# Gate/up and down as seven block products for eight, in groups of 1024 tokens with act kept in HBM

## Chip, cores and metric
One Trainium2 chip, one core. The metric is the device time of one execution, in microseconds; the kernel before has a median of 2003.85 us over three runs (2000.64 to 2003.87).

## What is computed
x has 2048 tokens of 1024 elements, in 8 sequences of 256. Each sequence has its own low-rank adapter (rank 16 of 16 sets). All is f32. The result is x + ffn(cond(x)):
```
gate = x @ Wg.T + 0.5 * (x @ Ag.T) @ Bg.T        # Wg: 2752 x 1024, per sequence Ag, Bg
up   = x @ Wu.T + 0.5 * (x @ Au.T) @ Bu.T
act  = silu(gate) * up                           # 2048 x 2752
y    = act @ Wd.T + 0.5 * (act @ Ad.T) @ Bd.T    # 2048 x 1024
top  = top_k(y @ W_gate + b_gate, 2)             # of 8 experts
out  = x + mean over the two of relu(y @ W_e[e] + b_e[e])
```

## The kernel before
The precision of f32 comes from splitting each operand into a high part (rounded to TensorE's fast f32 form, on ScalarE) and a low part (operand less high part, on VectorE): every block product is three matrix products, high x high, high x low and low x high (`first`, lines 1001 to 1003, and `mm3`, lines 953 to 955). A "product" below is one such TensorE instruction of 128 rows and 512 columns.

Four groups of 512 tokens (`NG`) follow one another. In gate/up, 22 chunks of 128 rows of Wg and Wu (`first`) are multiplied with x of the group, 8 blocks of 128 along the depth, 24 products to a chunk; the last chunk of each, 64 rows, shares one. x, split, stays in SBUF (`x_t`), and so does act of the group (`act_t`). ScalarE takes silu (L549), VectorE multiplies (L562), ScalarE and VectorE split act (L573, L582). Adapter products have 256 columns: `lora_in` (L962, 32 per group), `lora_out` (L974, 88), `lora_down_in` (L1022, 86). In down (`down`), two halves of 512 output columns each go over 11 weight pieces for four blocks of 128 tokens. y goes to HBM by `store_y`.

Weights come in pieces of 128 x 1024 (512 KB): SP's queue loads them into three raw buffers (`load`, L232), ScalarE writes the high part into a ring of three (`split_hi`, L456), VectorE the low part (`split_lo`, L475). The ring is free again when TensorE has done with the piece (`s_pe`).

Logits of y: VectorE multiplies y by broadcast rows of the gate matrix and accumulates (`l_step`, L640), 64 steps of 512 columns per group, the last group 32; for the rest TensorE transposes four tiles (L1085) and multiplies them with the matrix (L1095). VectorE then picks the two experts, ranks of the first 12 token blocks are made early (`early_hots`), and the expert stage runs over blocks of 128 rows sorted by expert (`one`): 48 products and 8 transposes (L1143) a block, GpSimd gathers y (L380), takes the low part of the transposed block (L390), adds the bias (L400) and scatters (L408). Expert weights are split by VectorE into one of two sides of R (L944, L945); those of expert 0 and three pieces of expert 1 are split in the last group (`EARLY`).

The order on ScalarE, VectorE and GpSimd is made by `Jobs`: each job has a key, the number of the weight piece at which it is due, and the engine runs them in order of key. An engine that waits in one job holds all that follow.
```
    def run(self, eng):
        for _, _, fn, args in sorted(self.jobs, key=lambda j: j[:2]):
            fn(eng, *args)
```


## Time and profile before

| | us |
|---|---|
| median of three runs | 2003.85 |
| span of the profiled execution, first to last instruction | 1998.1 |
| profiled execution's own time | not given apart; one of 2000.64, 2003.85 and 2003.87 |
| TensorE busy | 1971.3 (99%) |
| VectorE, ScalarE, GpSimd busy | 889.5, 629.5, 498.1 |
| HBM read and written, MB | 248.75, 36.70 |

The page comes from one execution. A busy share is a mean over stages; a TensorE duration is that of one instruction from its start to its modelled end, and overlaps with the next. The distance between starts is what an instruction costs. The granted clock of 1.0 is 2.4 GHz.

### The profile page before, as it was taken

The page shows a single profiled execution, that of the slowest core. Times are in us where ns is not written, and L with a number is a line of the kernel's source. Part 1 is how long each engine was busy: PE and PEld are TensorE (multiplying, and loading weights), DVE is VectorE, ACT ScalarE, POOL GpSimd, SP SyncE. Part 2 cuts the span into 40 slices and gives each one's busy share as a digit, 9 for nine tenths or more (in the row PEclk, how much of TensorE's full clock was granted, in tenths as well). Part 3 has the DMA queues.
Part 4 walks back from the last instruction along what each step waited for, and adds up shares of the span by engine and source line. Part 5 has one row for each costly group of instructions (what it writes and reads, how often), then busy time and mean ns, then how long its engine had stood idle before and what let it go on. Part 6 is the DMA issues. An engine that isn't in the chain of part 4 may idle for free.

```text
span 1998.1 us, 24457 instructions
## 1 busy us (share of the span) xinstructions
PE 1971.3 (99%) x9247; PEld 1644.4 (82%) x9247; DVE 889.5 (45%) x1293; ACT 629.5 (32%) x775; POOL 498.1 (25%) x373
## 2 busy tenths in 40 slices
PE   8999999999999999999999999999999999999997
PEld 6888888888888888888888888888888788888886
DVE  4333343255555423555553255555656443444310
ACT  4332332233233322323333232232332233333332
POOL 3111100011111001111110021111001666666664
PEclk9999999999999999999999999999999999999999
DMA  6433335344333442444344345433454566766543
GB/s 194 140 122 106 112 129 165 99 138 161 122 121 124 140 143 90 156 159 128 119 138 146 116 136 160 128 119 114 161 186 148 131 185 179 188 182 176 154 98 59
DMA packets 82802, 278.19 MB, mean 139 GB/s; under 512 B 11760, under 2 KB 12144, under 8 KB 82544
## 3 DMA queue, kind: packets, MB, share of 16 engines
q1 hardware_dynamic: 59472, 197.53, 30.2%
q0 software_dynamic: 23216, 79.05, 15.1%
q8 instruction: 82, 1.34, 0.3%
q14 instruction: 32, 0.26, 0.0%
HBM read 248.75 MB, written 36.70 MB: 143 GB/s over the span
## 4 chain that ended last, share of the span: by engine, by line
PE 98%; DVE 1%; issue 0%; DMA 0%; POOL 0%; SPq 0%; ACT 0%; POOLq 0%
PE PS L1002 16%; PE PS L1001 16%; PE PS L1003 16%; PE PS L953 14%; PE PS L955 14%; PE PS L954 14%; PE PS L974 2%; PE PS L1022 2%; PE PS L1143 2%; PE PS L962 1%; PE PS L1072 0%; PE PS L1050 0%; PE PS L1051 0%; DMA raw<-in_xp 0%; PE PS L1095 0%
## 5 line engine op out<-in xcount | busy, mean ns | idle before, releaser
L475 DVE TENSOR_TENSOR ring<-raw,ring 128x1024 fp32r<-128x1024 f32 x259 | 317.5, 1226 | 544.0 <-ACT ring L456 543.9
L1001 PE MATMUL PS<-R,ring 128*128 128x512 f32 x1376 | 538.3, 391 | 9.1 <-DVE R L468 6.4
L1002 PE MATMUL PS<-R,ring 128*128 128x512 f32 x1376 | 538.8, 392 | 0.0
L1003 PE MATMUL PS<-R,ring 128*128 128x512 f32 x1376 | 538.0, 391 | 0.0
L308 POOL DMA_INDIRECT AB<-in_bgu,idx_b x176 | 165.9, 943 | 898.7 <-DVE R L517 869.2
L456 ACT ACTIVATE ring<-raw 128x1024 fp32r<-128x1024 f32 x259 | 272.8, 1053 | 300.8 <-PE PS L955 292.0
L1001 PEld LDWEIGHTS PS<-R,ring 128*128 128x128 f32 x1376 | 259.4, 189 | 59.5 <-DVE R L468 6.4
L1003 PEld LDWEIGHTS PS<-R,ring 128*128 128x128 f32 x1376 | 259.0, 188 | 55.4
L1002 PEld LDWEIGHTS PS<-R,ring 128*128 128x128 f32 x1376 | 259.4, 188 | 49.1
L953 PE MATMUL PS<-ring,R 128*128 128x512 f32 x672 | 262.1, 390 | 0.0
L954 PE MATMUL PS<-ring,R 128*128 128x512 f32 x672 | 261.7, 389 | 0.0
L955 PE MATMUL PS<-ring,R 128*128 128x512 f32 x672 | 261.6, 389 | 0.0
L953 PE MATMUL PS<-R,ring 128*128 (+1 forms) x592 | 235.4, 398 | 2.5 <-issue 2.5
L955 PE MATMUL PS<-R,ring 128*128 (+1 forms) x592 | 231.9, 392 | 0.0
L954 PE MATMUL PS<-R,ring 128*128 (+1 forms) x592 | 231.4, 391 | 0.0
L573 ACT ACTIVATE R<-sbuf 128x512 fp32r<-128x512 f32 x88 | 55.6, 632 | 412.1 <-DVE sbuf L562 408.7
L944 DVE CAST R<-raw 128x1024 fp32r<-128x1024 f32 x53 | 66.1, 1246 | 200.0 <-PE PS L955 182.3
L640 DVE CUSTOM_DVE_ANT_0 PS<-ybuf,ytp 128x512 f32<-128x512 f32 x224 | 148.6, 719 | 0.0
L955 PEld LDWEIGHTS PS<-ring,R 128*128 128x128 f32 x672 | 126.1, 188 | 26.3
L954 PEld LDWEIGHTS PS<-ring,R 128*128 128x128 f32 x672 | 126.3, 188 | 26.0
L953 PEld LDWEIGHTS PS<-ring,R 128*128 128x128 f32 x672 | 126.2, 188 | 25.9
L953 PEld LDWEIGHTS PS<-R,ring 128*128 128x128 f32 x592 | 111.9, 189 | 25.6 <-issue 3.7
(152 smaller groups left out, 1704.5 us busy)
## 6 DMA issues: line engine op xcount, KB each, us to landing
raw<-in_wp SPq DMA_DIRECT2D x259, 512.0 KB, 3.5
raw<-in_we SPq DMA_DIRECT2D x64, 512.0 KB, 5.5
ytp<-in_wgb SPq DMA_DIRECT2D x56, 256.0 KB, 3.7
y_scratch<-ybuf POOLq DMA_DIRECT2D x7, 1024.0 KB, 6.7
raw<-in_xp SPq DMA_DIRECT2D x13, 512.0 KB, 3.6
AB<-in_be SPq DMA_DIRECT2D x8, 512.0 KB, 4.1
AB<-in_bgu,idx_b POOLq DMA_INDIRECT x176, 3.1
ybuf<-in_xp SPq DMA_DIRECT2D x2, 512.0 KB, 7.3
```

Source lines behind the costliest of these rows:

```text
L308: e.indirect_dma_start(out=braw[:, n % 2, b * 256:(b + 1) * 256], out_offset=None, in_=bgu, in_offset=ioa(idx_b[0:96, 2 * g + b, i:i + 1]) ...
L456: e.activation(piece_dst(i, 0), raw_t(i), ACT.Copy).then_inc(s_hi, 1)
L475: e.tensor_tensor(piece_dst(i, 1), raw_t(i), piece_dst(i, 0), ALU.subtract).then_inc(s_lo, 1)
L573: e.activation(act_t(c, 0)[0:p, :], sbuf2[0:p, 2 + c % 2, :], ACT.Copy).then_inc(s_ah, 1)
L640: e.tensor_tensor_reduce(out=PS[:, (5 if g < NG - 1 else 1) + n % 3, :], in0=ybuf[:, tt, h * 512:(h + 1) * 512], in1=ytp[:, (s % 2) * 512: ...
L944: link(e.tensor_copy(s_w_t(ex, k, 0), raw[:, i % RW, :]))
L953: e.matmul(out_, hi, whi, start=start, stop=False)
L954: e.matmul(out_, hi, wlo, start=False, stop=False)
L955: return e.matmul(out_, lo, whi, start=False, stop=stop)
L1001: e.matmul(PS[:, bank, :], w[0][:, sl], x_t(0, k), start=(k == 0), stop=False)
L1002: e.matmul(PS[:, bank, :], w[0][:, sl], x_t(1, k), start=False, stop=False)
L1003: e.matmul(PS[:, bank, :], w[1][:, sl], x_t(0, k), start=False, stop=False)
```

## The change
Two groups of 1024 tokens. Each is cut in two halves of 512 tokens, the depth of 1024 in two halves of 512, and the weight rows in pairs of chunks of 128. A pair of chunks with both token halves is a 2 x 2 by 2 x 2 block product, made with seven block products and sums of blocks (Winograd's form): `unit`. Even units are gate, odd ones up; unit 20 has gate and up of chunk 20. The 64 remaining rows go in plain products (`half_unit`).

A unit's made weight blocks S1 to S4 come from four GpSimd steps (`mix_w`); the made x blocks T1 to T4 of group 0 from VectorE and GpSimd at the start, those of group 1 through HBM (`mix`, four GpSimd steps in each of 14 rounds in units 3 to 16 of group 0, which also make four blocks of the down weights). Of the seven products each is accumulated into one of four PSUM banks; ScalarE copies a bank out (`e_copy`), TensorE goes on in it, VectorE adds (`c_add`).

act of a group has the same form in down: GpSimd makes four act blocks per pair of units (`mix_act`), seven are stored to HBM (`act_store`, on SP's queue) and come back as 35 pieces per group (`load_a`), split anew by ScalarE and VectorE (`a_hi`, `a_lo`). Down has seven stages (`STAGES`) of five pieces, 24 products each, and remainders of depth 192 in plain products (`rem`) in four of them. The down weights' low parts move from VectorE to GpSimd (`d_lo`).

The logits of the second 512 tokens of each group are made by TensorE with transposes and sums (`turn2`, `sum2`), 8 tiles of each; the first 512 stay on VectorE, 64 steps, in stages 2 to 5 (`l_key`). Stores of y, copies of x, and all other plain transfers are issued from SP's queue, which has an order by keys too. The keys now count block products: 228 to a group (`op`), gate/up at 0 to 149, down from 150 on, two to a piece. The weight ring has six slots of 512 columns. Of the expert weights only expert 0 is split early. In the diff, `st`, `tile`, `slot` and the like are buffers; `s_...` are semaphores.
```diff
-NG = 4
+NG = 2
 NC = 22
-NU = 65
-S2 = 43
+NP = 21
...
+OPS = 228
...
+D0 = 150
+NM = 39
+STAGES = 7
+FIRST_M = [0, 5, 11, 16, 21, 27, 33]
...
+        def load_a(e, j):
...
+            e.dma_start(raw_a(j), act_d[g, s, a].rearrange("p a n -> p (a n)")).then_inc(s_ra[jj % 3], 16)
...
+        def act_store(e, g, p):
...
+            for s, t, what, v in ((0, AT_T, s_mu, g * 44 + 4 * p + 1), (1, AT_T + 2, s_mu, g * 44 + 4 * p + 3),
+                                  (5, AT_T + 3, s_mu, g * 44 + 4 * p + 4), (3, SP_T, s_Sa, 4 * n + 1),
+                                  (6, AT_T + 1, s_Sa, 4 * n + 2), (2, SP_T + 1, s_Sa, 4 * n + 3),
+                                  (4, SP_T + 2, s_Sa, 4 * n + 4)):
+                e.wait_ge(what, v)
+                e.dma_start(act_d[g, s, p // 2, :, p % 2, :], tile(t)).then_inc(s_st, 16)
...
+        for j, (o, h) in enumerate([(0, 0), (0, 1), (2, 0), (2, 1), (1, 0), (1, 1), (3, 0), (3, 1)]):
+            sp.add(-29 + j, load_x0, o, h)
+        sp.add(-28.5, constants, False)
+        sp.add(-26.5, load, 1)
...
+            sp.add(7.0 * (r + 3) + 0.3, mix_load, r)
+            sp.add(7.0 * (r + 3) + 5.3, mix_store, r)
...
+                sp.add(op(g, 7 * (2 * p + 1)) + 11.3, act_store, g, p)
...
+        def l_key(g, o):
+            if o < 32:
+                return stage_end(g, 1) + 0.6 + 0.55 * o
+            return stage_end(g, 4) + 0.6 + 0.3 * (o - 32)
...
+        def mix_w(e, g, q):
...
+            if q:
+                e.wait_ge(s_lo, lo_of(g, 7 * (q - 1) + 5))
...
+            e.tensor_tensor(tile(S_T), a[1][0], a[1][1], ALU.add).then_inc(s_S, 1)
+            e.wait_ge(s_S, n + 1)
+            e.tensor_tensor(tile(S_T + 1), tile(S_T), a[0][0], ALU.subtract).then_inc(s_S, 1)
+            e.wait_ge(s_S, n + 2)
+            e.tensor_tensor(tile(S_T + 2), a[0][1], tile(S_T + 1), ALU.subtract).then_inc(s_S, 1)
+            e.tensor_tensor(tile(S_T + 3), a[1][0], a[0][0], ALU.subtract).then_inc(s_S, 1)
...
+        def mix_act(e, g, p):
...
+            e.wait_ge(s_mu, g * 44 + 4 * p + 4)
...
+            e.tensor_tensor(tile(SP_T), tile(AT_T + 1), tile(AT_T + 3), ALU.add).then_inc(s_Sa, 1)
+            e.wait_ge(s_Sa, n + 1)
+            e.tensor_tensor(tile(AT_T + 1), tile(AT_T + 1), tile(AT_T), ALU.subtract).then_inc(s_Sa, 1)
+            e.tensor_tensor(tile(SP_T + 1), tile(SP_T), tile(AT_T), ALU.subtract).then_inc(s_Sa, 1)
+            e.wait_ge(s_Sa, n + 3)
+            e.tensor_tensor(tile(SP_T + 2), tile(AT_T + 2), tile(SP_T + 1), ALU.subtract).then_inc(s_Sa, 1)
...
+        def mix(e, r):
+            e.wait_ge(s_cl, 64 * (r + 1))
+            e.tensor_tensor(st[0], st[1], st[0], ALU.subtract).then_inc(s_cp, 1)
...
+            e.tensor_tensor(st[1], st[1], st[3], ALU.subtract).then_inc(s_cp, 1)
...
+            e.tensor_tensor(st[3], st[3], st[0], ALU.subtract).then_inc(s_cp, 1)
...
+            e.tensor_tensor(st[2], st[2], st[3], ALU.subtract).then_inc(s_cp, 1)
...
+        def x0_t3(e, h):
...
+            e.wait_ge(s_xt, h + 1)
+            e.wait_ge(s_q[6 + h], 16)
+            e.tensor_tensor(X0[1][:, hs], X0[1][:, hs], X0[3][:, hs], ALU.subtract).then_inc(s_xp, 1)
...
+        def d_lo(e, g, m):
...
+            e.tensor_tensor(slot2(n, 1), pair(raw_t(i)), slot2(n, 0), ALU.subtract).then_inc(s_lp, 1)
...
+                pool.add(op(g, 7 * q) - 5.4, mix_w, g, q)
...
+                pool.add(op(g, 7 * (2 * p + 1)) + 8.4, mix_act, g, p)
...
+                pool.add(op_m(g, m) - 6 + 0.55, d_lo, g, m)
...
+            pool.add(7.0 * (r + 3) + 3.0, mix, r)
...
+            pool.add(-6 + 0.1 * h, x0_t3, h)
+            pool.add(-5.6 + 0.1 * h, x0_t4, h)
...
+        def w_hi(e, g, n):
...
+                e.wait_ge(s_S, (g * NP + q) * 4 + j - 1)
+            hi_free(e, op(g, n))
+            e.activation(slot(op(g, n), 0), w_src(g, n), ACT.Copy).then_inc(s_hi, 1)
+        def w_lo(e, g, n):
+            e.wait_ge(s_hi, g * (LO1 + 2 * NM) + n + 1)
+            e.tensor_tensor(slot(op(g, n), 1), w_src(g, n), slot(op(g, n), 0), ALU.subtract).then_inc(s_lo, 1)
...
+        def a_lo(e, j):
+            e.wait_ge(s_ah, j + 1)
+            e.tensor_tensor(a_ring(j, 1), raw_a(j), a_ring(j, 0), ALU.subtract).then_inc(s_al, 1)
...
+        def e_copy(e, g, q, k):
...
+            e.wait_ge(s_pe, pe_op(g, 7 * q + [0, 2, 3, 5][k]))
...
+            e.activation(tile(E_T + [0, 1, 2, 0][k]), PS[:, bk + [0, 2, 0, 0][k], :], ACT.Copy).then_inc(s_ec, 1)
...
+        def c_add(e, g, q, k):
...
+            e.tensor_tensor(c_tile(q, k), tile(E_T + [0, 2, 0, 1][k]), PS[:, bk + [1, 2, 3, 0][k], :],
+                            ALU.add).then_inc(s_c, 1)
...
+            e.tensor_tensor_reduce(out=JK[n % 2], in0=tile(SET_C + tt),
...
+                key = op(g, n) - 5.6
+                act.add(key, w_hi, g, n)
+                dve.add(key + 0.15, w_lo, g, n)
...
+                    act.add(n0 + [1.05, 3.05, 4.05, 6.05][k], e_copy, g, q, k)
...
+                    dve.add(due, c_add, g, q, k)
...
+            def lora1_in(g):
...
+                for w in range(2):
...
+                    src = ([("B11", 0), ("B21", 4)], [("T1", 0), ("B11", 0), ("B22", 4)])[w]
+                    for i in range(2):
...
+                        todo = [(o, k0, k, part) for o, k0 in src for k in range(4) for part in range(2)]
...
+            def unit(g, q):
...
+                main1(g, n0, "B11", bk, True, True).then_inc(s_pe, 1)
...
+                m = main1(g, n0 + 1, "B21", bk + 1, True)
...
+                main1(g, n0 + 2, "T1", bk + 2, True, True).then_inc(s_pe, 1)
...
+                if q == 0:
+                    lora1_in(g)
...
+                e.wait_ge(s_ec, ec + 1)
+                main1(g, n0 + 3, "T2", bk, False, True).then_inc(s_pe, 1)
...
+                e.wait_ge(s_ec, ec + 2)
+                main1(g, n0 + 4, "B22", bk + 2, False)
+                m = lora1_out(g, q, 0, 1, bk + 2)
...
+                e.wait_ge(s_ec, ec + 3)
+                main1(g, n0 + 5, "T3", bk, False, True).then_inc(s_pe, 1)
...
+                main1(g, n0 + 6, "T4", bk + 3, True)
+                e.wait_ge(s_ec, ec + 4)
+                lora1_out(g, q, 1, 1, bk)
+                lora1_out(g, q, 1, 0, bk + 3).then_inc(s_pe, 1)
...
+            def half_unit(g):
...
+                main1(g, 147, "B11", 4, True, True).then_inc(s_u1, 1)
+                main1(g, 147, "T1", 5, True).then_inc(s_pe, 1)
...
+                main1(g, 148, "B22", 5, False)
...
+                main1(g, 148, "B21", 4, False)
...
+            def piece(g, s, kp):
...
+                e.wait_ge(s_al, j + 1)
...
+                e.wait_ge(s_lp, g * NM + m_ + 1)
...
+                        m = mm3(PS[:, bank(s, i), :], a_ring(j, 0)[:, o:o + 128], a_ring(j, 1)[:, o:o + 128],
+                                slot(G + a, 0), slot(G + a, 1), start=(kp == 0 and a == 0),
+                                stop=(kp == 4 and a == 1 and s not in (1, 4, 5)))
...
+            def rem(g, s, i):
...
+                mm3(o, act20(0, w)[:, ts], act20(1, w)[:, ts], slot(G, 0), slot(G, 1), start=False)
+                e.matmul(o, act21(w)[:, ts], slot(G + 1, 0), start=False, stop=False, skip_group_check=True)
+                return e.matmul(o, act21(w)[:, ts], slot(G + 1, 1), start=False, stop=False, skip_group_check=True)
...
+            def tail2(g, s):
...
+                        e.wait_ge(s_ev, ev_of(g, 6, i))
...
+            for m in range(8):
+                sum2(1, m)
+                if m < 6:
+                    turn2(1, m + 2)
```

## Rows read from the trace of the kernel before

**Rows 1.** The page: busy time by engine, and the granted clock in 40 slices
```profile
PE 1971.3 (99%) x9247; PEld 1644.4 (82%) x9247; DVE 889.5 (45%) x1293; ACT 629.5 (32%) x775; POOL 498.1 (25%) x373
...
PEclk9999999999999999999999999999999999999999
```

**Rows 2.** The chain in order of time (start us, us, what)
```profile
17.97 3.81 PE PS L962 x32
...
1157.66 3.82 PE PS L962 x32
...
1590.10 0.87 PE PS L1143 x8
1601.90 0.87 PE PS L1143 x8
```

**Rows 3.** Order of time, TensorE: transposes, a sum, the first expert transposes
```profile
1531.60 0.60 PE L1085 MATMUL PS<-ident,ybuf 128*128 128x128 f32 x4
...
1535.06 0.96 PE L1095 MATMUL PS<-wg_s,ytp 128*128 128x8 f32 x8
...
1538.11 1.07 PE L1143 MATMUL PS<-ident,sbuf 128*128 128x128 f32 x8
```

**Rows 4.** Two stretches: busy us of each engine, clock, DMA share, GB/s
```profile
0.00:18.00 18.00, 8.93 (x26) 6.67 (x27) 9.48 (x14) 9.35 (x11) 8.77 (x12) 0.91 0.85 280
760.00:1140.00 380.00, 380.00 (x1768) 317.50 (x1768) 181.98 (x292) 116.16 (x152) 50.16 (x53) 1.00 0.41 133
```

**Rows 5.** Groups by line and shape, TensorE: busy us, mean ns, idle before
```profile
L1001 PE MATMUL PS<-R,ring 128*128 128x512 f32 x1376 | 538.3, 391 | 9.1 <-DVE R L468 6.4 <-DVE R L475 2.7
L974 PE MATMUL PS<-TT,R 96*128 96x256 f32 x352 | 69.5, 283 | 0.0
```

**Rows 6.** Groups by line and shape, the other engines
```profile
L475 DVE TENSOR_TENSOR ring<-raw,ring 128x1024 fp32r<-128x1024 f32 x259 | 317.5, 1226 | 544.0 <-ACT ring L456 543.9
L456 ACT ACTIVATE ring<-raw 128x1024 fp32r<-128x1024 f32 x259 | 272.8, 1053 | 300.8 <-PE PS L955 292.0 <-DMA raw<-in_wp 5.4 <-PE PS L1072 3.4
L640 DVE CUSTOM_DVE_ANT_0 PS<-ybuf,ytp 128x512 f32<-128x512 f32 x224 | 148.6, 719 | 0.0
L390 POOL TENSOR_TENSOR ring<-ytp,ring 128x1024 fp32r<-128x1024 f32 x36 | 88.4, 2456 | 45.6 <-ACT ring L720 45.4
L517 DVE TENSOR_TENSOR R<-AB,R 32x512 fp32r<-32x512 f32 x104 | 70.3, 680 | 3.1
L582 DVE TENSOR_TENSOR R<-sbuf,R 128x512 fp32r<-128x512 f32 x84 | 58.2, 693 | 58.7 <-ACT R L573 58.7
L562 DVE TENSOR_TENSOR sbuf<-sbuf,PS 128x512 f32<-128x512 f32 x84 | 57.8, 688 | 119.0 <-PE PS L974 118.8
L549 ACT ACTIVATE sbuf<-PS 128x512 f32<-128x512 f32 x84 | 50.2, 597 | 259.7 <-PE PS L974 259.7
L640 DVE DVE_READ_ACCUMULATOR2_ANT Lp<- 128x1 f32 x224 | 31.7, 141 | 0.0
```

**Rows 7.** Order of time, TensorE, the start
```profile
8.23 0.63 PE L1002 MATMUL PS<-R,ring 128*128 128x512 f32 x1
8.65 0.63 PE L1003 MATMUL PS<-R,ring 128*128 128x512 f32 x1
```

**Rows 8.** The page, DMA issues: KB each, median us to landing
```profile
raw<-in_wp SPq DMA_DIRECT2D x259, 512.0 KB, 3.5
```

**Rows 9.** Order of time, GpSimd and VectorE, around 1550 and 1716 us
```profile
1550.23 2.20 POOL L362 TENSOR_TENSOR ybuf<-ybuf,cf 128x656 bf16<-128x656 bf16 x1 [0.78 <-DVE ybuf L912]
...
1716.11 2.39 POOL L400 TENSOR_TENSOR sbuf<-sbuf,AB 128x1024 f32<-128x1024 f32 x1 [0.87 <-ACT sbuf L728]
1716.28 3.31 DVE L945 TENSOR_TENSOR R<-raw,R 128x1024 fp32r<-128x1024 f32 x1
```

**Rows 10.** Order of time, VectorE between expert 1 and expert 2
```profile
1572.94 1.23 DVE L945 TENSOR_TENSOR R<-raw,R 128x1024 fp32r<-128x1024 f32 x1
1596.50 0.69 DVE L944 CAST R<-raw 128x1024 fp32r<-128x1024 f32 x1 [22.33 <-PE PS L955]
```

More of the change, by code:

```diff
@@ new lines, in build @@
+        for i in range(i, len(pieces)):
+            _, e, k = pieces[i]
+            if (e, k) in ((1, 0), (1, 2)):
+                sp.add(keys[i], load_bias, k // 2)
+            if e >= 2 and k == 3:
+                sp.add(keys[i], load_bias, e)
+            sp.add(keys[i], load, i)
+        for h in range(2):
+            sp.add(op_m(0, 33) + 0.1, load_x1, h)
+        for j in range(70):
+            g, jj = divmod(j, 35)
+            m = FIRST_M[jj // 5] + jj % 5
+            sp.add(max(op_m(g, m) - 6 - 5.3, op(g, 144.4 if jj < 2 else 147.3)), load_a, j)
@@ L707, in blk_hi @@
+        for h in range(2):
+            dve.add(-4.5 + 0.01 * h, x0_t1, h)
+            dve.add(-3.5 + 0.01 * h, x0_t2, h)
+        for k in range(8):
+            act.add(keys[at["e", 0, k]], e_hi, k)
+            dve.add(keys[at["e", 0, k]] + 0.1, e_lo, k)
         def blk_hi(e, b):
@@ new lines, in early_table @@
+            def early_table():
+                e.wait_ge(s_ee, 1)
+                for t in range(ET):
+                    m = e.matmul(EP[:, 32:36], e_or[:, t, :], e_ob[:, t].rearrange("p a b -> p (a b)"),
+                                 start=(t == 0), stop=(t == ET - 1))
+                m.then_inc(s_ep, 1)
+            for g in range(NG):
+                for q in range(NP):
+                    unit(g, q)
+                half_unit(g)
+                for s in range(STAGES):
+                    for kp in range(5):
+                        piece(g, s, kp)
+                        if g == NG - 1 and s == 6 and kp == 1:
+                            early_ranks()
+                        if g == NG - 1 and s == 6 and kp == 3:
+                            early_table()
+                    if s in REM_M:
+                        tail2(g, s)
```

1624 lines of the change are left out of this document (1036 added, 588 removed).

## The prediction, made before the changed kernel was run
> **What bounds the kernel now.** I read the page first: the busy shares, the slices, then the chain that ended last. TensorE is busy for 99% of the span, its share is at 9 in all slices but the first and the last, and the granted clock stands at 1.0, the 2.4 GHz level, from end to end [rows 1]. The chain in order of time shows the period: the adapter product of a token group starts at 17.97 and, three groups on, at 1157.66, so a group takes 379.9 us, and the expert stage's first transposes start at 1538.1 [rows 3]. The table by stretches says that nothing but TensorE is near a limit: in a whole group it is busy for 380.0 of 380.0 us, VectorE for 182, ScalarE for 116, GpSimd for 50 [rows 4]. So time comes off only if TensorE gets less to do, and the question is whether the others can then still feed it.
>
> **TensorE's work.** A group of 512 tokens has 43 x 24 products of 512 columns in gate/up and 2 x (21 x 4 x 3 + 4 x 2 + 4) in down, 1560 in all, and 32 + 88 + 86 = 206 adapter products of 256 columns. 32 of the latter take 3.82 us, 0.119 each [rows 2]; (379.9 - 24.5) / 1560 = 0.2278 us per product of 512 columns. (The mean duration of 391 ns [rows 5] overlaps with the next one and is no price.)
> After, a group of 1024 tokens has 21 units of 7 x 12 products, 48 in the half unit, 7 x 5 x 24 in down, 4 x 4 x 5 for the remainders and 16 adapter outputs: 2748. Two groups have 5496 against 4 x 1560 = 6240: 744 fewer x 0.2278 = **-169.5 us**. Adapter products of 256 columns: 80 + 176 + 172 = 428 per group, 856 against 824, **+3.8**. Half of the logits leave VectorE's accumulating multiply for TensorE: 16 transposed tiles and sums against 4. One tile costs 0.60 for its transposes and 0.96 for its sum [rows 3]: 12 x 1.56 = **+18.7**.
>
> **The start.** Before, the adapter input begins at 17.97 behind 24 products (5.5 us), so the pace counts from 12.5. After, it stands behind three products, and the third (T1 times a made weight block) has a long way: GpSimd's queue holds both halves of T3 and T4 ahead of the first weight mix. Ten transfers of 512 KB come first; at the 280 GB/s of the first 18 us [rows 4] each takes 1.9, so x block 12 is whole at about 17 and block 22 at about 21. VectorE makes T1 (1.23 a half), GpSimd T3 (2 x 2.46), VectorE the low parts of T1 and B22 and then T2, GpSimd T4 (2 x 2.46) and then S1 [rows 6]; with VectorE and GpSimd excluding each other (below) I get 36 for S1, 38 for the third product, a pace that counts from 38 - 5.5 = 32.5, 20 us later than before. While TensorE had gaps before, the rows show products 0.43 apart instead of 0.23 (half clock, 1.2 GHz) [rows 7]; +2. **+22**. Bounds: 10 if nothing excludes anything and the transfers go faster; 35 with each half mix at the upper price below and a cold clock throughout.
>
> **Boundaries.** Group 1 starts only when all four sums of the last stage are out of PSUM: 4 x 0.69 behind the last product, where before the waits are in my 0.2278; the same at the end of group 1; with the first act blocks coming back from HBM (store, load of 3.5 us [rows 8], split of 1.05 and 1.23, all inside the 11.4 us of the half unit) I take **+5** (2 to 12). The first adapter outputs wait for four ScalarE copies of about 1 us and a VectorE step, with two products (5.4 us) as cover: **+2** for two groups. The end of group 1 has eight transposes and sums in a chain with ScalarE copies of 0.6: **+3** (1 to 8).
>
> **The lock between VectorE and GpSimd.** Here lies the risk. A VectorE subtraction of 1024 columns with both inputs in SBUF takes 1.23; the one that started 0.17 us behind a GpSimd one took 3.31: it stood until GpSimd's 2.39 were over [rows 9]. The Trainium skill (SBUF — State Buffer, "SBUF: two separate sides") calls this an exclusive lock on a shared port pair, held for the whole instruction, by GpSimd's operations and by VectorE's with two SBUF inputs. If it were no lock the next two paragraphs would cost nothing, and the sum would be 22 us lower; the row agrees with the lock. In the kernel before, GpSimd only gathers in this stage; after, it does the mixes of weights, of act and, in group 0, of the made operands, and half of the splits of down.
> Price of a 512-column step: VectorE 0.69 both ways, 0.68 for 32 partitions, ScalarE 0.60 [rows 6]. No row has GpSimd at 512 columns of f32. Below is half of 2.46, 1.2; above the 2.20 of 656 bf16 columns with a broadcast input [rows 9], 1.7 for 512. I take 1.31, half of 2.46 and the 0.08 that VectorE's half (0.69) has over half of its 1.23. The Trainium skill (GPSIMD Engine Reference, "Reconciling with measured numbers") gives 4.5 us at 2048 columns; with the row at 1024 that line would make it an estimated 1.33.
>
> **Gate/up units.** A unit lasts 84 x 0.2278 + 8 x 0.119 = 20.1 us. In it the lock is held by VectorE for 7 low parts, 2 gatings, 2 adapter rows (7.6) and by GpSimd for 4 weight mixes and 2 act mixes (7.9), in units 3 to 16 of group 0 for 4 more (13.1 in all, the sum 20.7). That is just over the unit. The order of the queues makes it sharper: ScalarE's split of the next unit's S1 is queued ahead of its copy of this unit's fourth product, and TensorE's sixth product waits for that copy. So S1 has to be there 12.9 us into the unit (5 products of 2.86, less 1.3 for split and copy). In even units GpSimd mixes act first: sums, adapter rows and gating end at 3.8, five GpSimd steps follow: 10.4 alone, 13.8 if each stands behind one VectorE step. I take half a microsecond for 20 even units and 2 more in the first group's busy ones, **+12** (0 to 121, below). Gathers are fewer (4 per pair of units for 2 per unit) and wider; GpSimd is busy with them for 50 of 380 us before [rows 4], and they fit.
>
> **Down.** A piece is 24 products, 5.5 us, 6.4 with adapter input; GpSimd's split takes 2.46, VectorE's 1.23, ScalarE's two 1.05 each: alone they fit. While logit steps run (0.72 under the lock and 0.14 [rows 6]; 32 are due in 52 us of stages 2 and 3, 32 in 32 us of stage 5) the lock is asked for 32 x 0.72 + 8.8 x 3.7 + 4.4 x 1.23 = 61 us of 52, and 23 + 5 x 3.7 = 41.5 of 32: some 9 us behind each time. Rings of three give a VectorE split 8.5 us of slack (two pieces less its own steps). So the stall is small: 2.5 in each of four windows, **+10** (0 to 50).
>
> **The expert stage** keeps its 11.8 us per block [rows 2]. It has three fewer pieces of expert 1 split beforehand, some 3 x 3 us on VectorE; it now ends them at 1574 and then idles 22.33 us until expert 0 is done [rows 10]. Covered, 0. The early ranks take VectorE 6 us inside two pieces (10.9): 0. Copying x is moved to SP's queue, ahead of loads with 9 us or more of slack: 0. HBM traffic: 86 MB of weights (164 pieces of 0.524) for 136 (260 pieces), and new are act out and in (73 MB) and the made operands (29 MB), 52 MB more over some 1440 us, 36 GB/s on top of 133 [rows 4], and about 225 in the busiest units against 280 shown: 0.
>
> **Sum**: -169.5 + 3.8 + 18.7 + 22 + 5 + 2 + 3 + 12 + 10 = -93 on a span of 1998.1. The profiled execution's own time isn't given apart; the median is 5.75 above the span, and I take that as what lies around it: 1905.1 + 5.75 = **1911 us**.
>
> **Rivals.** (a) The covers hold: no unit stalls, no window stalls, start +15: -122, **1882**. For it: all averages but one are below their limits. Against: the order in even units. (b) The forecast. (c) The lock costs more than my middle, the units 40 and the windows 30: -45, **1959**. (d) Slower: GpSimd's step is at its 1.7. Then S1 is ready at 3.8 + 5 x (1.7 + 0.69) = 15.8, 2.9 late in 20 even units, 58, and the busy units ask for 17 + 7.6 = 24.6 us of lock in 20.1, 4.5 x 14 = 63: 121 for the 12, so +16, **2020**. It decides from a step of about 1.65 us. Against it: a GpSimd step of 1024 f32 columns at 2.39, with nothing broadcast. That the seven products aren't a real saving is ruled out by the count. (e) No change needs 93 us of further stalls by chance.
> The chances: (a) 0.28, (b) 0.40, (c) 0.19, (d) 0.11, (e) 0.02. The range reaches from (a) with its best start, 1862, through (c) to 1970. About 0.2%, 4 us, is what a measurement of this kernel can tell from no change: faster 0.87, same 0.02, slower 0.11. The likeliest case alone: 1890 to 1935.
>
> **What would show it.** TensorE with 5496 products of 512 columns at 0.228 apart; the adapter input of group 0 starting at about 41; units of 20 to 21 us in group 1, up to 23 in the even units 4 to 16 of group 0; GpSimd's 512-column steps at 1.3; VectorE subtractions of 0.69 stretched to about 2 beside GpSimd; TensorE's waits put down to ScalarE's copies and low parts; the first expert transposes at about 1445. I am wrong if units are at 24, if TensorE's clock leaves 1.0 in gate/up, or if transfers are what ends its waits.

## The result and the profile after

The change makes the kernel slower: 2059.82 us (median of four runs, 2055.79 to 2063.94) against 2002.24 (2000.33 to 2003.87), ratio 1.0289, 95% interval 1.0270 to 1.0309. I had said 1911, 1862 to 1970. In the profiled executions the span goes from 1998.1 to 2060.6, up by 62.5 where my sum had it down by 93: the miss is 155 us. (By the medians it is 149: the profiled execution, 2062.44, is 1.8 above its span, where I had put 5.75.)

The page of the kernel after (busy time; clock in 40 slices; chain by engine and line):
```profile
PE 1882.0 (91%) x8679; PEld 1560.7 (76%) x8679; DVE 1141.9 (55%) x1355; ACT 744.0 (36%) x1054; POOL 1083.1 (53%) x659
...
PEclk8899999999899998899999999899998899999999
...
PE 66%; DVE 7%; issue 6%; DMA 6%; POOL 5%; ACT 3%; SPq 0%; ACTq 0%; DVEq 0%; POOLq 0%
```
TensorE has less to do, as forecast, but is busy for 91% instead of 99% [rows 1], its clock has dips, and the chain now leads through every engine and the DMA. Four stretches, with the columns of [rows 4]: the start, units 8 and 9 of group 0, and unit 18 of group 1:
```profile
0.00:18.00 18.00, 5.52 (x13) 3.91 (x13) 9.17 (x13) 6.44 (x7) 6.21 (x10) 1.00 0.82 319
...
242.40:268.80 26.40, 23.06 (x95) 18.67 (x94) 19.25 (x18) 9.27 (x16) 21.56 (x16) 0.87 0.83 301
268.80:288.90 20.10, 20.10 (x95) 16.76 (x94) 12.54 (x14) 7.92 (x14) 14.08 (x10) 1.00 0.50 171
...
1233.20:1253.80 20.60, 20.40 (x94) 16.70 (x93) 14.80 (x16) 8.97 (x16) 14.59 (x10) 1.00 0.48 160
```
Unit 9, at 268.8, takes 20.1 us, what I worked out for 84 products and 8 adapter products: the arithmetic saved is real. Unit 8, at 242.4, takes 26.4, TensorE idle for 3.3 of it and at a mean clock of 0.87. So I cut the trace at the first product of 512 columns of each unit and piece; such a table says where the time went:

| stretch, us | after | best of the runs below |
|---|---|---|
| group 0, unit 0 | 68.4 | 51.5 |
| group 0, units 1 to 20 | 458.4 | 402 |
| group 1, unit 0 | 60.8 | 51.5 |
| group 1, units 1 to 20 | 415.9 | 402 |
| two half units | 44.7 | 25.7 |
| stage 3's first piece and stage 5's remainder, both groups | 68.3 | 28.8 |
| the rest of down | 453.5 | 443 |

(The right-hand column isn't free of waits: the two units 0 would take 29.6 and 42.1 by the count of products alone, an estimate from 0.2278 and 0.119 us each and, in group 1, eight tiles of logits at 1.56.) Five kinds of wait make the difference. **Even units of group 0**; order of time on GpSimd, ScalarE, TensorE in unit 8:
```profile
242.83 1.62 POOL L653 TENSOR_TENSOR FT<-FT 128x512 f32<-128x512 f32 x1
247.19 0.90 POOL L691 DMA_INDIRECT brw<-in_bgu,idx_b  x1 [2.74 <-DVE R L975]
...
255.34 1.15 ACT L970 ACTIVATE R<-brw 96x512 fp32r<-96x512 f32 x2 [2.56 <-DMA brw<-in_bgu,idx_b]
256.39 0.57 ACT L1029 ACTIVATE FT<-PS 128x512 f32<-128x512 f32 x1
...
257.11 0.77 PE L1571 MATMUL PS<-R,ring 128*128 128x512 f32 x1 [3.34 <-ACT FT L1029]
257.67 0.63 PE L1572 MATMUL PS<-R,ring 128*128 128x512 f32 x1
258.10 0.63 PE L1573 MATMUL PS<-R,ring 128*128 128x512 f32 x1
```
ScalarE's copy of the third block product (L1029) has its input from about 251, but stands in the queue behind the adapter rows' splits (L970), which wait for gathers issued at 247.2 and 248.4, behind GpSimd's mixes and a wait for VectorE; the second landed 6.9 us later. TensorE needs those rows only at the end of the fifth block product, the copy at its start. And behind its wait its products stand 0.43 us apart (1.2 GHz) instead of 0.23.

**Unit 20 and the half unit** (ScalarE, then TensorE): the same with act's first piece, which comes back from HBM:
```profile
533.52 1.06 ACT L849 ACTIVATE R<-FT 128x1024 fp32r<-128x1024 f32 x1 [3.81 <-DMA FT<-act_scratch]
536.46 0.63 ACT L1062 ACTIVATE FT<-FT 128x512 f32<-128x512 f32 x1 [1.89 <-DVE FT L1057]
537.00 0.58 ACT L1029 ACTIVATE FT<-PS 128x512 f32<-128x512 f32 x1
...
537.63 1.23 PE L1616 MATMUL PS<-R 96*128 96x256 f32 x4 [6.38 <-ACT FT L1029]
```
**Group 1's unit 0** (ScalarE, TensorE): T4 back from HBM ahead of a logit copy (L1166):
```profile
843.45 2.00 ACT L880 ACTIVATE R<-raw 128x1024 fp32r<-128x1024 f32 x2 [10.28 <-DMA raw<-xt_scratch]
845.36 0.58 ACT L1166 ACTIVATE ytp<-PS 128x512 f32<-128x512 f32 x1
...
845.99 1.88 PE L1829 MATMUL PS<-wg_s,ytp 128*128 128x8 f32 x8 [9.23 <-ACT ytp L1166]
```
**The start** (TensorE, GpSimd). The third product starts at 38.83, where I had 38. But then there is a second wait, behind the second half of the adapter rows (ScalarE waits 10.3 us for their gather) and the copies queued after them, and later GpSimd stands still for 22.7 us behind the store of an adapter row that it gathers by way of HBM:
```profile
38.83 0.80 PE L1571 MATMUL PS<-R,ring 128*128 128x512 f32 x1 [17.92 <-DVE ring L834]
...
68.09 0.77 PE L1571 MATMUL PS<-R,ring 128*128 128x512 f32 x1 [11.39 <-issue]
...
89.58 0.94 POOL L680 DMA_INDIRECT ytp<-in_agu,idx_a  x1 [22.69 <-DMA ad_scratch<-ytp]
```
**The windows of the logit steps** (chain in order of time): two of the logit steps (L1205), 0.69 us each alone, take 2.8 and 3.1 beside GpSimd's splits, and the adapter's low part (L1011) is queued behind all of them:
```profile
769.67 2.83 DVE FT L1205
...
774.34 3.10 DVE FT L1205
...
784.92 0.69 DVE R L1011
785.61 0.04 issue
785.65 2.08 PE PS L1789 x4
```
The groups of the other engines show the lock [rows 6, 9] in its means: splits of act pieces take 2236 ns instead of 1226, of weight blocks 982 and 1065 instead of 693; GpSimd's four weight steps take 1.43 to 1.71:
```profile
L834 DVE TENSOR_TENSOR ring<-FT,ring 128x512 fp32r<-128x512 f32 x168 | 164.4, 982 | 180.3 <-ACT ring L830 177.7
L853 DVE TENSOR_TENSOR R<-FT,R 128x1024 fp32r<-128x1024 f32 x70 | 156.5, 2236 | 186.7 <-ACT R L849 186.5
L834 DVE TENSOR_TENSOR ring<-raw,ring 128x512 fp32r<-128x512 f32 x130 | 138.3, 1065 | 121.9 <-ACT ring L830 121.5
...
L626 POOL TENSOR_TENSOR FT<-raw 128x512 f32<-128x512 f32 x42 | 71.7, 1706 | 0.0
...
L621 POOL TENSOR_TENSOR FT<-raw 128x512 f32<-128x512 f32 x42 | 60.2, 1433 | 176.3 <-DMA raw<-in_wp 149.9 <-issue 20.6 <-DVE ring L834 5.7
```

### The profile page after: what moved, and what is told of

Read it like the earlier page. It is cut to its first block, busy times and chain, and to the rows that moved or that the text cites. A ratio compares the mean times of both kernels' runs of the same rounds, so it can differ in the third digit from the quotient of the medians.

```text
span 2060.6 us, 24701 instructions
## 1 busy us (share of the span) xinstructions
PE 1882.0 (91%) x8679; PEld 1560.7 (76%) x8679; DVE 1141.9 (55%) x1355; ACT 744.0 (36%) x1054; POOL 1083.1 (53%) x659
## 4 chain that ended last, share of the span: by engine, by line
PE 66%; DVE 7%; issue 6%; DMA 6%; POOL 5%; ACT 3%; SPq 0%; ACTq 0%; DVEq 0%; POOLq 0%
PE PS L1571 20%; PE PS L1572 19%; PE PS L1573 19%; DVE FT L1205 3%; DMA brw<-in_bgu,idx_b 3%; PE PS L1878 2%; PE PS L1616 2%; PE PS L1710 1%; DMA ytp<-in_wgb 1%; POOL brw L691 1%; DMA raw<-in_wp 1%; ACT R L970 1%; PE PS L1829 1%; ACT R L849 1%; DVE R L853 1%
## 5 line engine op out<-in xcount | busy, mean ns | idle before, releaser
L1571 PE MATMUL PS<-R,ring 128*128 128x512 f32 (+1 forms) x1800 | 724.9, 403 | 83.6 <-DVE ring L834 30.4
L1572 PE MATMUL PS<-R,ring 128*128 128x512 f32 (+1 forms) x1800 | 715.1, 397 | 0.0
L1573 PE MATMUL PS<-R,ring 128*128 128x512 f32 (+1 forms) x1800 | 714.1, 397 | 0.0
L1571 PEld LDWEIGHTS PS<-R,ring 128*128 128x128 f32 x1800 | 346.8, 193 | 161.4 <-issue 52.8
L1573 PEld LDWEIGHTS PS<-R,ring 128*128 128x128 f32 x1800 | 346.1, 192 | 75.6
L1572 PEld LDWEIGHTS PS<-R,ring 128*128 128x128 f32 x1800 | 347.6, 193 | 66.4
L712 POOL TENSOR_TENSOR ring<-raw,ring 128x1024 fp32r<-128x1024 f32 x78 | 192.5, 2467 | 360.6 <-ACT ring L840 357.5
L834 DVE TENSOR_TENSOR ring<-FT,ring 128x512 fp32r<-128x512 f32 x168 | 164.4, 982 | 180.3 <-ACT ring L830 177.7
L853 DVE TENSOR_TENSOR R<-FT,R 128x1024 fp32r<-128x1024 f32 x70 | 156.5, 2236 | 186.7 <-ACT R L849 186.5
L830 ACT ACTIVATE ring<-FT 128x512 fp32r<-128x512 f32 x168 | 105.9, 631 | 300.0 <-PE PS L1616 130.1
L834 DVE TENSOR_TENSOR ring<-raw,ring 128x512 fp32r<-128x512 f32 x130 | 138.3, 1065 | 121.9 <-ACT ring L830 121.5
L840 ACT ACTIVATE ring<-raw 128x1024 fp32r<-128x1024 f32 x78 | 82.7, 1061 | 334.2 <-PE PS L1573 309.7
L1571 PEld LDWEIGHTS PS<-ring,R 128*128 128x128 f32 x592 | 113.5, 192 | 44.2 <-DVE FT L1151 18.6
L975 DVE TENSOR_TENSOR R<-brw,R 32x512 fp32r<-32x512 f32 x88 | 99.3, 1148 | 69.2 <-ACT R L970 68.1
L1573 PEld LDWEIGHTS PS<-ring,R 128*128 128x128 f32 x592 | 113.1, 191 | 24.5
```

Of the source, the lines that this page charges most:

```text
L712: e.tensor_tensor(slot2(n, 1), pair(raw_t(i)), slot2(n, 0), ALU.subtract).then_inc(s_lp, 1)
L830: e.activation(slot(op(g, n), 0), w_src(g, n), ACT.Copy).then_inc(s_hi, 1)
L834: e.tensor_tensor(slot(op(g, n), 1), w_src(g, n), slot(op(g, n), 0), ALU.subtract).then_inc(s_lo, 1)
L840: e.activation(slot2(n, 0), pair(raw_t(i)), ACT.Copy).then_inc(s_hi, 2)
L853: e.tensor_tensor(a_ring(j, 1), raw_a(j), a_ring(j, 0), ALU.subtract).then_inc(s_al, 1)
L975: e.tensor_tensor(m, b_raw(p, t)[32:64], m, ALU.subtract).then_inc(s_bl, 1)
```

## Experiments

Three theories: A, the order of the queues; B, the lock and GpSimd's steps; C, transfers. "Dense" is the start of the last remainder of group 1, the last point before the expert stage: 1581.8 after the change. It matters because the runs on 16 columns leave out arithmetic, compute other logits and so have one or two expert blocks fewer (8623 and 8567 TensorE instructions for 8679, 56 to a block; the expert stage takes 446.4 and 436.7 us for 459.9). The time that a theory gave is set beside theirs with those 14 or 23 us added; for the rest only their dense part is compared.

### One thing at a time
**Adapter rows' splits later**
```diff
-  key = op(g, 14 * p) + [[-1.6, 2.6], [0.1, 2.6]][t][w]
+  key = op(g, 14 * p) + [[-1.6, 3.1], [0.1, 3.1]][t][w]
```


> One number: from the second pair of units on, the splits of the adapter rows of the T path (ScalarE and VectorE) are queued at 3.1 instead of 2.6 products into the even unit, so behind ScalarE's copy of the third product and no longer ahead of it. Nothing else moves. Theory A (order of the queues): in group 0 TensorE's wait in even units is that copy, held up behind a row gather that lands late; the fifth product needs the rows only at its end. Then the excess of units 1 to 20 of group 0 over 20.08 us falls from 57 us to about 30, and the time from 2060 to about 2025. Theory B (the lock between VectorE and GpSimd): what is late are the split weights themselves; the copy was only the first to show it. Then the units stay within 0.5 us of what they are and the time at 2055 to 2065. Theory C (transfers): the gathers land late because HBM and queues are full; the excess falls as in A, but landings stay at 7 to 8 us.

2051.58 us; dense 1571.8, 10 less. Units 1 to 20 of group 0 fall from 458.4 to 449.4. The copy is no longer late, and the low part of the rows (L975) takes its place, 0.9 to 1.3 us in most even units and 6.5 in unit 12: the gather itself is late. 9 us of the 27 that A promised in these units.

**GpSimd on 16 columns**
```diff
+  c = 16 if n else 512
...
-  e.tensor_tensor(tile(S_T), a[1][0], a[1][1], ALU.add).then_inc(s_S, 1)
+  e.tensor_tensor(tile(S_T)[:, 0:c], a[1][0][:, 0:c], a[1][1][:, 0:c], ALU.add).then_inc(s_S, 1)
...
```


> Leaves out most of the arithmetic: every two-input step of GpSimd before the expert stage (weight mixes, act mixes, made operands, low parts of the down weights) works on 16 columns of each 512 instead of all, but for the first unit's weight mix. Instructions, waits, transfers and queue orders are the same. It takes GpSimd's load and with it the lock away, and nothing else. Theory B (the lock is the cause of all): VectorE's steps are back at 0.69 and 1.23, units of both groups at 20.1, half units at 12, no window stalls; only the start and the act round trip stay: 1895 to 1910. Theory A (order of the queues is the cause, the lock its trigger): the even units of group 0 are at 20.1 to 20.6 too, since the gathers are then issued in time, but unit 20, the half unit and the stage with 32 logit steps in 27 us keep part of their waits, since there a load stands ahead in a queue: 1920 to 1950. Theory C (transfers): even units of group 0 keep over half of their excess of 57 us, since all bytes still move: above 1960.

1976.2 us, some 1990 with the missing block; dense 1508.1, 74 less: B and A had promised far more, only C's bound (above 1960) holds. The windows give the largest part (68.3 to 37.2), units 1 to 20 of group 0 give 23 of 57 and the half units 5, unit 20 and group 1's unit 0 next to nothing. The run takes away GpSimd's own long steps and the lock together, so the two together are one half of the matter at most, and unit 12 at 29.9 looked like C.

**Logit steps spread**
```diff
-  return stage_end(g, 1) + 0.6 + 0.55 * o
-  return stage_end(g, 4) + 0.6 + 0.3 * (o - 32)
+  return stage_end(g, 1) + 0.6 + 0.9 * o
+  return stage_end(g, 4) + 0.6 + (0.4 if g else 0.55) * (o - 32)
```


> VectorE's 64 logit steps per group are due further apart: the first 32 every 0.9 products instead of 0.55, the second 32 every 0.55 (group 0) and 0.4 (group 1) instead of 0.3; the loads of the router's rows follow them, and group 1's T2 is loaded 6 products later. The work is the same. Theory A: the windows stall because four steps use up a row block in 3.4 us of stage 5 while a block's round trip is 5 to 7 us with two buffers, so VectorE waits for loads with the adapter's low part queued behind. Then the two waits of 13.9 us at the remainder of stage 5 nearly go in group 0 and halve in group 1, those at the first piece of stage 3 (8.8 and 7.9) fall to under 3, and the time to about 2025. Theory B (the lock's demand in VectorE and GpSimd): the demand is the same in the stage as a whole, so the waits shrink by less than a third: above 2045.

2040.72 us; dense 1559.6, 22 less; the four windows 38.1 for 68.3, some 11 of it lost again to steps that stand in other places. The waits fall as A said, the time by 19 us of the 35 it had: an order fixes what the lock brought to light.

**Made operands on 16 columns**
```diff
-  e.tensor_tensor(st[0], st[1], st[0], ALU.subtract).then_inc(s_cp, 1)
+  e.tensor_tensor(st[0][:, 0:16], st[1][:, 0:16], st[0][:, 0:16], ALU.subtract).then_inc(s_cp, 1)
...
```


> Leaves out most of the arithmetic of the made operands alone (the 14 rows of combined down weights and x blocks that GpSimd makes in units 3 to 16 of group 0): 16 columns of each 512. Their loads and stores all stay. Theory B and A alike: even units 4 to 16 of group 0 are at 20.6 as in group 1, about 30 us gone, 2025 to 2030; where A holds, gathers land in 3 to 5 us after they are due. Theory C (the 29 MB of loads and stores of these rows crowd out gathers and weights): the even units keep their 22 to 26 us and gathers their landing of 7 to 8 us, above 2045.

2024.42 us, but two expert blocks fewer, so some 2048 with them, in C's range; dense 1567.0, 15 less. Half of what A and B said; unit 12 stays at 28.1.

**Copies of x later**
```diff
-  sp.add(60 + 14.0 * n, copy_x, n)
+  sp.add(op(1, 60) + 14.0 * n, copy_x, n)
```


> The five copies of x into the output (four of 2 MB) are issued in units 8 to 16 of group 1 instead of group 0; all else as in the changed kernel. Theory C' (transfers at one place: each copy is issued on SP's queue in an even unit, ahead of that unit's seven act stores, and a weight load and a row gather stand in its traffic): even units 8, 10, 12, 14, 16 of group 0 lose most of what they have over units 4 and 6 (unit 12 falls from 30.5 to 22 or 23 us), about 15 to 20 us; in group 1, where no made operands are in the way, the copies cost under 8 us: 2045 to 2052. Theory A (the copies are as harmless as I put them, at 0): unit 12 stays at 28 to 30 us and the time at 2058 to 2062.

2055.9 us; dense 1578.7, 3 less. Unit 12 falls by 5 us, units 6 and 10 rise by 4 each. In group 1 the copies cost nothing. By the time C' misses and my 0 for the copies was near enough, though unit 12 fell below A's 28.

**The start and the row gathers**
```diff
-  pool.add(op(g, 7 * q) - 5.4, mix_w, g, q)
+  pool.add(op(g, 7 * q) - (5.4 if g or q else 6.1), mix_w, g, q)
-  pool.add(4.2 + 2 * r, gather_row, r)
+  pool.add(5 + 3.6 * r, gather_row, r)
-  sp.add(7.0 * (r + 3) + 0.3, mix_load, r)
+  sp.add(7.0 * (r + 5) + 0.3, mix_load, r)
...
```


> Three orders of the first units, same work: the eight adapter row gathers that go through HBM (gather, store, next gather, one buffer) are due every 3.6 products from the 5th instead of every 2 from the 4.2nd, and the made operands two units later; the first weight mix goes ahead of GpSimd's T3 and T4; the second half of the first B rows is gathered ahead of the second weight mix and split behind the adapter input's copies. Theory A (queue orders): the page's wait of 22.7 us of GpSimd for a store of such a row is what delays the second and third weight mix; unit 0 falls from 68.4 to about 55 us (third product at about 34, the 11.4 us gone), units 1 to 3 from 75.6 to about 63: 2030 to 2040. Theory B (lock and GpSimd's time): with one more unit of made operands beside act mixes the units later get what the first ones save: above 2050.

2043.89 us; dense 1564.5, 17 less. Unit 0 at 59.6, units 1 to 3 at 69.4 for 75.6. Then units 4 to 19 take 4 more: the time lies between the ranges of A (2030 to 2040) and B (above 2050).

### Orders and lock, each with and without the other
**All orders**: the above, and
```diff
-  key = op_m(g, FIRST_M[jj // 5] + jj % 5) - 5.55
+  key = max(op_m(g, FIRST_M[jj // 5] + jj % 5) - 5.55, op(g, [146.1, 147.65, 149.1][min(jj, 2)]))
-  key = op(g, 147.2)
+  key = op(g, 147.6)
...
-  key = op(1, 0) + 0.1 + 0.1 * h if o == "T2" else keys[at["x", o, h]]
+  key = op(1, 0) + 0.1 + 0.1 * h if o == "T2" else op(1, 0) + 2.1 + 0.05 * h if o == "T4" else keys[at["x", o, h]]
```


> All order changes together (the adapter rows' splits later, logit steps spread, start and row gathers, x copies in group 1), and two new: in unit 20 and the half unit the act block's and the adapter's splits stand behind ScalarE's copies that TensorE waits for, and in group 1's unit 0 the splits of T4 stand behind the first two logit copies. No work is left out and none is added. Theory A: unit 20 at 21 to 23 (27.6 and 29.4 before), the half unit at 15 (22.4), group 1's unit 0 at 48 (60.8), windows as in the spread run, start as in the run before: 194 us of excess come down to 70 to 90, 1945 to 1965, faster than the kernel before the change. Theory B (the lock and GpSimd's time set a floor near the count of its demand): no lower than 1990.

1975.47 us, ratio 0.9868 (0.9846 to 0.9890): the sign of the change turns with nothing but keys. Unit 20 is at 20.1 in both groups, the half units at 27.6 together for 44.7, group 1's unit 0 at 52.2. That is 10 us above A's range, 15 below B's bound.

**The same on 16 columns**

> The run with all orders (1975), with GpSimd's two-input steps on 16 columns of 512 as in the earlier run with 16 columns: leaves most of that arithmetic out. With the orders of the change this was worth 84 us. Theory A (the lock costs time where an order leaves no slack, and little once the orders are mended): now it is worth less than half of that, 20 to 35 us, mostly at the start and in units 6 to 18 of group 0: 1940 to 1955. Theory B (orders and lock are two separate sums): it is again worth 60 to 85 us: 1890 to 1915.

1895.69 us, some 1910 with the missing expert block: in B's range (1890 to 1915), below A's. The dense part in the four kernels:

| dense, us | change's orders | all orders | orders give |
|---|---|---|---|
| GpSimd whole | 1581.8 | 1496.7 | 85 |
| GpSimd on 16 columns | 1508.1 | 1426.9 | 81 |
| 16 columns give | 74 | 70 | |

In the whole the two sums add up, so this is not one cause with a trigger. By stage it is less clean: in units 1 to 20 of group 0 the orders alone give 22, the 16 columns alone 23, both 56; in down it is 21, 42 and 48. With both gone, every unit of group 0 from 1 to 20 but one is at 20.1, unit 12 at 20.5, with all bytes still moving: transfers alone, C, cost nothing. What late landings (6.9 us for a gather of unit 8, a median of 3.1 in the kernel before) add where an order leaves no room was not taken apart.

**More orders**
```diff
+ROW_AT = [10.4, 12.7, 18.4, 24.4, 26.7, 32.4, 38.0, 40.3]
-  act.add(op(g, 3.0), t1_hi, g)
+  act.add(op(g, 3.07), t1_hi, g)
...
```


> The run with all orders, with two more: at the start VectorE and ScalarE split S1 and block 22 ahead of the adapter's own rows, and the adapter input's copies stand behind ScalarE's copy of the third product; the eight row gathers through HBM stand in the stretches of a unit in which neither GpSimd's mixes nor SP's loads are due (units 1 to 5), the made operands one unit later. Same work. Theory A (what is left at the start and in units 3 and 5 is order too): third product at 27 to 30 instead of 35.6, unit 0 at 50 (60.4), units 3 and 5 at 21 to 22 (28.1 and 24.8), the rest as there: 1950 to 1960. Theory B (GpSimd's and VectorE's time is used up in these units): the time comes back in the units behind, 1970 or more.

1958.05 us, ratio 0.9778 (0.9758 to 0.9798); the third block product starts at 27.5, unit 0 is at 55.6, units 1 to 3 at 60.8, down by 13 together, and nothing is paid back behind (units 4 to 19 at 341.8 for 347.9). Dense 1479.8, 17 less: A.

### No work on GpSimd but gathers
**The change with the steps on VectorE**
```diff
-  pool.add(op(g, 7 * q) - 5.4, mix_w, g, q)
+  DV.append((op(g, 7 * q) - (3.7 if g and q == 1 else 4.9 if g or q else 4.2), mix_w, g, q))
-  pool.add(op(g, 7 * (2 * p + 1)) + 8.4, mix_act, g, p)
+  DV.append((op(g, 7 * (2 * p + 1)) + 8.4, mix_act, g, p))
-  pool.add(op_m(g, m) - 6 + 0.55, d_lo, g, m)
+  DV.append((op_m(g, m) - 6 + 0.55, d_lo, g, m))
...
+  for a in DV:
+      dve.add(*a)
```


> The changed kernel with that move alone, in the change's own orders. Theory B: its excess by GpSimd's steps (89 us by the first 16-column run) goes to the larger part, all else stays: 1975 to 2000, no slower than the kernel before the change. Theory A: 2030 or more, since the orders of the change with loads waited for in VectorE's queue are worse than in GpSimd's.

1992.86 us, ratio 0.9963 (0.9946 to 0.9980), dense 1515.7: 66 of the 74 us that leaving the arithmetic out had given, with no arithmetic left out: B. (The weight mixes and T3 and T4 are also due at slightly other keys.)

**The same with the second set of orders**

> The second run of orders (1958), with all two-input steps that GpSimd does before the expert stage (weight, act and made mixes, T3, T4, low parts of the down weights) moved to VectorE's queue at the same places but for the weight mixes, half a product later. No arithmetic is left out; GpSimd only gathers. VectorE gets some 0.69 us for each step of 1.3 to 1.7 on GpSimd: 17.3 us of 20.1 in the busiest units, where both together ask for over 20 now. Theory B (exclusion: a GpSimd step costs the pair twice what it costs on VectorE, and 79 us of time hang on it): most of the gain of the 16-column run comes without leaving work out: units 1 to 20 of group 0 at 20.1 to 20.7, windows with logit steps 5 us better in sum: 1895 to 1925. Theory A (the pair shares the work well; what GpSimd's absence gave was its own slow steps' lateness, and VectorE in order is as late): VectorE's single queue waits for loads and products with splits behind it: 1950 or more.

1941.83 us, ratio 0.9701 (0.9684 to 0.9717). B had 1925 at most, A 1950 at least. Windows at 30.4, as B said, but unit 6 of group 0 is at 26.4 and even units 8 to 18 at 22.4 to 24.0, the latter each with a wait of 2.06 for the adapter rows' low part: VectorE's queue has the four steps of the made operands ahead of it.

**Those four steps behind it**
```diff
-  sp.add(7.0 * (r + 6) + 5.3, mix_store, r)
+  sp.add(7.0 * (r + 6) + 6.2, mix_store, r)
-  DV.append((7.0 * (r + 6) + 3.0, mix, r))
+  DV.append((7.0 * (r + 6) + 4.4, mix, r))
```


> The run with all on VectorE (1942), its four steps for a row of made operands due 1.4 products later in the unit and their stores 0.9 later: behind the adapter rows' low parts in VectorE's queue instead of ahead. Same work. There units 8 to 18 of group 0 took 24.0 in even ones, each with a wait of 2.06 us for those low parts, which stood behind the four steps (2.8 us). Theory A (order again, now in VectorE's queue): even units at 20.1 to 21.5, some 22 us less in six or seven units: 1915 to 1922. Theory B (VectorE's 17 us of work in such a unit are too much whatever the order, or the gather lands too late anyway): another wait takes its place and units stay above 22.5: 1930 to 1942.

1915.39 us (five runs), ratio 0.9569 (0.9556 to 0.9582): the fastest, 84 us under the runs of the kernel before beside it, and 4 us above the number I had given for the change, which is chance: it took new orders and a move of work to get there. Page and groups:
```profile
PE 1843.1 (96%) x8679; PEld 1536.8 (80%) x8679; DVE 1159.1 (61%) x1741; ACT 744.6 (39%) x1054; POOL 440.0 (23%) x273
...
PEclk8999999999999999999999999999998999999999
...
L836 DVE TENSOR_TENSOR ring<-FT,ring 128x512 fp32r<-128x512 f32 x168 | 115.8, 691 | 145.7 <-ACT ring L832 144.4
...
L855 DVE TENSOR_TENSOR R<-FT,R 128x1024 fp32r<-128x1024 f32 x70 | 85.4, 1220 | 9.8 <-ACT R L851 9.8
```
VectorE does 386 more instructions in 17 us more than after the change (1159.1 for 1141.9): its splits are back at 0.69 and 1.22, and the time that it had spent standing beside GpSimd now holds all that took GpSimd 643 us.

### Exclusion alone
**Idle steps**: the fastest version, with GpSimd steps that nobody waits for.
```diff
+  t = tile(ST_T)
+  for k in range(4):
+      if n + k:
+          e.wait_ge(s_idle, n + k)
+      e.tensor_tensor(t, t, t, ALU.subtract).then_inc(s_idle, 1)
...
+  for q in range(1, 20):
+      pool.add(op(1, 7 * q) + 1.5, idle_steps, q, 0)
+      if q >= 10:
+          pool.add(op(1, 7 * q) + 4.4, idle_steps, q, 1)
```


> The fastest version (1915) with steps on GpSimd that nobody waits for, in group 1 only: 4 subtractions of 128x512 f32 in one spare tile in each of units 1 to 9, and 8 (4 early, 4 later in the unit) in each of units 10 to 19. No result changes and no wait is added on another engine; the gathers stand behind them in GpSimd's queue. VectorE's steps with two SBUF inputs there take some 11.8 us of a unit of 20.1 (7 low parts, 4 weight mixes, 2 act mixes, 2 gatings, 2 adapter rows); 4 more steps of 1.3 make 17, 8 make 22.3. Theory B1 (exclusion alone costs time): units 1 to 9 at 20.1 to 20.7 with VectorE's steps stretched beside GpSimd's, units 10 to 19 at 22 or more: 10 x 2 = 20 us and more, 1930 to 1950. Theory B2 (what cost time was that the splits' own chain went through GpSimd's slow steps, not that VectorE stood still beside them): all units within 0.6 us of 20.1, 1914 to 1922.

1984.07 us, 69 more. Both sets of units are hit: even ones at 25.6 to 26.5 up to unit 9 and 28.1 to 29.7 from there, odd ones at 20.1. GpSimd's queue bunches the steps of two units into the even one, behind a gather: 8 in a row there up to unit 9, then 12 in a row and 4 more. GpSimd, VectorE, ScalarE and TensorE in order of time in unit 2:
```profile
805.86 11.19 POOL L727 TENSOR_TENSOR FT<-FT 128x512 f32<-128x512 f32 x8
...
805.56 1.91 DVE L640 TENSOR_TENSOR FT<-FT 128x512 f32<-128x512 f32 x1
807.50 1.41 DVE L642 TENSOR_TENSOR FT<-FT 128x512 f32<-128x512 f32 x1
808.84 1.52 DVE L643 TENSOR_TENSOR FT<-FT 128x512 f32<-128x512 f32 x1
810.40 1.41 DVE L645 TENSOR_TENSOR FT<-FT 128x512 f32<-128x512 f32 x1
...
813.18 0.68 DVE L1077 TENSOR_TENSOR FT<-FT,PS 128x512 f32<-128x512 f32 x1
...
813.89 0.63 ACT L1082 ACTIVATE FT<-FT 128x512 f32<-128x512 f32 x1 [4.35 <-DVE FT L1077]
814.43 0.58 ACT L1049 ACTIVATE FT<-PS 128x512 f32<-128x512 f32 x1
...
815.15 0.72 PE L1596 MATMUL PS<-R,ring 128*128 128x512 f32 x1 [3.62 <-ACT FT L1049]
```
Each 0.69 us step of VectorE with both inputs in SBUF gets one turn between two of GpSimd's and costs 1.4 to 1.5. The sum that reads PSUM (L1077) takes its 0.68 in the middle of a GpSimd step, but it is due behind the stretched ones; ScalarE's silu step waits for it, and the copy that TensorE waits for stands behind that one. Eight such steps of GpSimd cost TensorE 5.5 to 6.4 us in that unit. So steps of GpSimd that hand nothing to the splits' chain cost time by standing in VectorE's way, beyond B1's forecast, and again by way of an order. They did so where my count had 17 of 20.1 us as well: that is the mean of two units, and with eight steps in the even one the same count is 22.3. Whether the same steps spread evenly would cost less wasn't tried. (That nobody waits for the steps isn't quite so: gathers queue behind them, and ScalarE has a wait for the last of them ahead of a copy in down, when it is long done.) What GpSimd's slower steps in the splits' own chain would cost without exclusion stays open; it wasn't tried.

## Why the prediction was wrong

**The count and the pace: right.** Units where nothing is late take 20.08 us in both groups; the third block product starts at 38.83 for 38; the expert stage (459.9 us for 460.0 before), the bytes of HBM (54 MB more for 52) and the copies of x came as put or cost nothing. Even units of group 1 take 20.6, the half microsecond that I had put down, but by luck: with GpSimd on 16 columns they are at 20.6 still, and with the adapter rows' splits later at 20.1 (the odd ones then at 20.6), so it was ScalarE's order and not the lock. No run without waits reached rival (a)'s 1882: the run on 16 columns with all orders would be at some 1910 with its missing block.

**"Gathers are fewer [...] and wider; [...] they fit": the step that failed first.** I priced the adapter's gathers by GpSimd's time in them, and not by who stands in line behind one that is late. ScalarE's queue in order put TensorE's next input behind them in even units, behind act's first piece in unit 20, behind T4 in group 1's unit 0; GpSimd's queue put two weight mixes behind a 22.7 us wait for a row's store. I had looked for this once, for S1, and had that place right. What I took as boundaries, 5, and first adapter outputs, 2, measured some 9 (group 1's unit 0, 60.8 for 51.5) and 19 (half units, 44.7 for 25.7), and unit 20 another 17 in the two groups. (The best run's 51.5 for group 1's unit 0 is itself 9 above the count of 42.1, so the boundary is short by more than that.) All orders together: 85 us, by stage 31 in the windows, 22 and 9 in units 1 to 20 of the two groups, 17 in the half units, 8 and 9 in the units 0, less 10 lost in the rest of down.

**The start, 22 (10 to 35).** The pace counts from 50.6 at the second unit's start (80.2 less 29.6 for unit 0's own work), against 12.5: 38, past the upper bound. The step to the third product was right; the second wait, 11.39 for the second half of the adapter rows and copies queued behind them, wasn't in the sum.

**The lock, 12 + 10.** Right in kind, and the price of a GpSimd step was right where no VectorE step with two SBUF inputs is beside it (1.25 to 1.3 us for 1.31; 1.43 to 1.71 in the means above). The size was wrong: GpSimd's steps, by the lock and by their own length together, were worth 70 to 74 us, three times as much. How the two share it no run shows. I had set the demand against the length of a unit or window, 20.7 against 20.1, and taken the excess for the stall. The idle steps show that this is too little: with 22.3 of 20.1 asked for in the even units, 2.2 too much, they cost 5.5 to 6.4 us. My reading, not shown apart, is that steps in a bunch stretch all that a copy or split stands behind at once. In the windows the 61 of 52 us became 5.6 to 6.5 us of wait, and the 41.5 of 32 nearly 13 in each group, since the logit steps and the waits for their rows stand ahead of the one step that TensorE waits for. The Trainium skill (SBUF — State Buffer, "SBUF: two separate sides") calls the lock exclusive and held for the whole instruction. That the steps go in turn, and that the sum which reads PSUM isn't held up, agrees; the whole instruction does not quite: the idle steps take 1.05 us with no VectorE step beside them, VectorE's take 0.69, and a pair in turn takes 1.45 and not 1.74. The Trainium skill (GPSIMD Engine Reference, "Reconciling with measured numbers"), by which I had an estimated 1.33 for a step, is near: the mixes took 1.25 to 1.3 alone.

**TensorE's clock: I had named it as a sign, and priced it at 2 us.** After a wait the rows show products 0.43 us apart instead of 0.23. Counting the starts of 512-column products in the trace, 256 stand 0.30 to 0.47 behind the one before, and they take 44 us more than at 0.2278 each; in the fastest version 83, and 14 us; in the kernel before 34, and 6 us. The granted clock was half in 24 stretches, 192 us in all; before, in 3, 21 us. So some 40 of the 155 us are not waits but the pace behind them, inside the sums above.

**Rivals.** Slower had 0.11. The sign came out as (d), but not by its mechanism: its step of 1.65 us was nearly reached in the means, but it gave units 121 us, where they have 70 over their floor, 17 of them in the two units 20, which the 16 columns left as they were; the rest of the loss lay where I had no rival, in the queues. The lower bound of the range has no working either: (a) with its best start of 10 is 1877, not 1862.
